# Turning the expert blocks' tokens with a DMA transpose instead of TensorE

## The reference, cut to what matters

```python
logits = x @ router_w + router_b
probs = jax.nn.softmax(logits, axis=-1)
top_v, top_i = jax.lax.top_k(probs, TOP_K)
top_v = top_v / jnp.sum(top_v, axis=-1, keepdims=True)
...
gate = jnp.einsum('td,edi->eti', x, gate_w) + gate_b[:, None, :]
up = jnp.einsum('td,edi->eti', x, up_w) + up_b[:, None, :]
h = jax.nn.silu(gate) * up
expert_out = jnp.einsum('eti,eid->etd', h, down_w) + down_b[:, None, :]
y = jnp.einsum('te,etd->td', weights, expert_out)
```

## Time and profile before

| what | us |
|---|---|
| median of 3 executions | 355.83 |
| lowest, highest | 355.47, 358.65 |
| the profiled execution | 359.83 |
| its span, first to last instruction | 358.0 |
| block 4's first matmul to block 38's first matmul | 144.10 |

### The profile page before, as it was taken

How to read it: one execution, slowest core, us unless ns; L and a number is a source line. 1 busy time by engine, 2 the same in 40 slices (tenths; PEclk the granted TensorE clock), 3 DMA queues, 4 the chain that set the end, 5 groups by cost and what they waited for, 6 DMA issues and landing times.

```text
span 358.0 us, 11098 instructions
## 1 busy us (share of the span) xinstructions
PE 295.7 (83%) x3773; PEld 178.3 (50%) x3774; DVE 276.0 (77%) x569; ACT 209.9 (59%) x380; POOL 202.7 (57%) x176
## 2 busy tenths in 40 slices
PE   0596868878878755977989989999999999899970
PEld 0186435545545532322446556666666666566640
DVE  3998785989999996778658767888888878688750
ACT  0277688989999964277135435555555555455520
POOL 2833132786889889452233476575756575565451
PEclk9998975989999997885599999999999999999995
DMA  7450100355544457679126777977768687767942
GB/s 183 84 180 3 61 2 6 117 187 171 185 168 142 152 168 226 234 221 240 37 53 112 114 124 123 134 127 125 132 119 134 116 149 109 128 120 131 116 63 30
DMA packets 70656, 45.00 MB, mean 126 GB/s; under 512 B 47992, under 2 KB 63608, under 8 KB 70240
## 3 DMA queue, kind: packets, MB, share of 16 engines
q1 hardware_dynamic: 62368, 34.09, 37.4%
q0 software_dynamic: 7488, 10.39, 20.3%
q10 hardware_dynamic: 768, 0.14, 0.3%
HBM read 23.43 MB, written 9.63 MB: 92 GB/s over the span
## 4 chain that ended last, share of the span: by engine, by line
PE 41%; DVE 16%; DMA 13%; issue 11%; ACT 9%; POOL 4%; POOLq 2%; ACTq 0%; DVEq 0%
PE bank L862 15%; DMA out_dram<-w_stage,gate 8%; PE bank L885 7%; DMA w_stage<-token_rows,gate 4%; ACT kq L1040 3%; PE bank L679 3%; DVE maxes L1327 3%; PE bank L762 2%; PE bank L588 2%; PE bank L850 2%; PE bank L670 2%; DVE s_exp L1336 2%; POOLq L527 2%; PE bank L552 2%; DMA w_exp<-in_L_conv_pairs_dram 1%
## 5 line engine op out<-in xcount | busy, mean ns | idle before, releaser
L862 PE MATMUL bank<-w_exp,v_t 128*128 x468 | 113.6, 379 | 2.0 <-DVE v_t L1526 1.4
L534 POOL DMA_INDIRECT out_dram<-w_stage,gate x39 | 62.2, 1594 | 54.4 <-DMA out_dram<-w_stage,gate 32.5
L862 PEld LDWEIGHTS bank<-w_exp,v_t 128*128 128x128 f16 x468 | 45.9, 98 | 42.2 <-issue 4.2
L885 PE MATMUL bank<-w_exp,kq 128*128 x468 | 57.9, 273 | 1.0 <-DVE w_stage L1572 0.8
L520 POOL DMA_INDIRECT w_stage<-token_rows,gate x39 | 40.1, 1029 | 27.9 <-ACT gate L1131 11.2
L1152 ACT ACTIVATE kq<-w_stage 128x512 f16<-128x512 f32 x38 | 23.9, 630 | 53.8 <-DVE w_stage L1555 53.8
L885 PEld LDWEIGHTS bank<-w_exp,kq 128*128 128x128 f16 x468 | 45.6, 98 | 15.0 <-issue 1.1
L438 POOL TENSOR_TENSOR w_exp<-w_stage,w_exp 128x1024 f16<-128x1024 f32 x16 | 34.1, 2134 | 12.3 <-ACT w_exp L1051 12.3
L1562 DVE TENSOR_TENSOR kq<-w_stage,kq 128x512 f16<-128x512 f32 x38 | 26.3, 693 | 16.7 <-ACT kq L1152 16.7
L1547 DVE TENSOR_TENSOR kq<-bank,v_t 128x512 f32<-128x512 f32 x39 | 26.9, 691 | 11.4 <-PE bank L862 11.3
L1555 DVE TENSOR_TENSOR w_stage<-s_exp,kq 128x512 f32<-128x512 f32 x39 | 27.1, 694 | 3.9 <-DVE kq L1547 0.4
(11 more groups left out here) (255 smaller groups left out, 519.2 us busy)
## 6 DMA issues: line engine op xcount, KB each, us to landing
w_stage<-in_L_ffn_gate_w_dram SPq DMA_DIRECT2D x8, 512.0 KB, 3.6
w_stage<-in_L_ffn_up_w_dram SPq DMA_DIRECT2D x8, 512.0 KB, 3.4
w_stage<-in_L_ffn_down_w_dram SPq DMA_DIRECT2D x8, 512.0 KB, 3.6
x_rows<-in_x_dram SPq DMA_DIRECT2D x8, 256.0 KB, 5.9
out_dram<-x_rows SPq DMA_DIRECT2D x4, 512.0 KB, 6.1
v_t<-in_L_ffn_up_b_dram SPq DMA_DIRECT2D x2, 1024.0 KB, 10.6
token_rows<-z_stack SPq DMA_DIRECT2D x4, 512.0 KB, 6.4
z_two<-z_stack SPq DMA_DIRECT2D x6, 256.0 KB, 2.4
```

The lines of the kernel that those rows point to most:

```text
L534: pool.indirect_dma_start(out, bass.IndirectOffsetOnAxis(t_scatter[:, b:b + 1], 0), yw[b % 2], None, compute_op=ALU.add).then_inc(s[f"y_la ...
L862: mm = pe.matmul(GU[par][k][:], xs[par][:, c, :], w_exp[:, w * W_EXP + k * W_PIECE + c * FF:][:, bass.ds(e, FF)], start=(n == 0), stop=(n ...
L885: mm = pe.matmul(YB[:, 0:L_COL], hs[par][:, c, :], w_exp[:, w * W_EXP + 2 * W_PIECE + c * L_COL:][:, bass.ds(e, L_COL)], start=(n == 0), s ...
```

## The change

Tokens are no longer turned by TensorE, save those of blocks 0 and 1. ScalarE and VectorE split a block's tokens as they lie, by rows, into one tile of 128 x 512 fp16 (high half, low half), and SyncE turns that tile with a third DMA transpose per block, issued after the two of the hidden product. There are four token buffers in place of two, and 6 gathers ahead in place of 5. On ScalarE `weigh` of n-3 moves behind `silu` of n, and tokens and share are those of block n+2. `yw` moves to another place in memory. The zeros are written by GpSimd itself, on the scatters' semaphores, whose counts all rise by one DMA; a scatter before which no scatter must have landed now waits for none (before, scatter 1 waited for scatter 0, and scatter 2 and all later ones for one scatter of each buffer).

```diff
-            sp.wait_ge(s["zero_ready"], 1)
-            for i in range(2):
-                sp.dma_start(out[TOKENS + SLOT * i:TOKENS + SLOT * (i + 1), :], ws_flat[:, 0:L_COL])\
-                    .then_inc(s["pad_out"], 16)
...
+            def turn_tokens(b):
+
+                sp.wait_ge(s["xl_ready"], b + 1)
+                sp.wait_ge(s["gu_ps"], 2 * (b - 1))
+                sp.dma_start_transpose(x_turned[b % 2], x_rows_h[b % 2]).then_inc(s[f"xt_in{b % 2}"], 16)
+
+            turn_tokens(2)
             for b in range(BLOCKS - 1):
                 turn_hidden(b)
+                if b + 3 < BLOCKS:
+                    turn_tokens(b + 3)
...
             table(pool.memset(ws_flat[:, 0:L_COL], 0.0))
-            pool.sem_inc(s["zero_ready"], 1)
+            for i in range(2):
+                pool.dma_start(out[TOKENS + SLOT * i:TOKENS + SLOT * (i + 1), :], ws_flat[:, 0:L_COL])\
+                    .then_inc(s[f"y_landed{i}"], 16)
...
             def gather(b):
 
-                if b >= 2:
-                    pool.wait_ge(s["share_ready"], b - 1)
-                pool.indirect_dma_start(xg[b % 2], None, token_rows,
+                if b >= 4:
+                    pool.wait_ge(s["share_ready"], b - 3)
+                    pool.wait_ge(s["xl_ready"], b - 3)
+                pool.indirect_dma_start(xg[b % 4], None, token_rows,
...
-                landed = [pool.value_load(t_landed[i][0:1, b:b + 1], min_val=16, max_val=8 * BLOCKS + 8)
-                          for i in range(2)] if b >= 2 else []
+                landed = [pool.value_load(t_landed[i][0:1, b:b + 1], min_val=16, max_val=8 * BLOCKS + 24)
+                          for i in range(2)] if b >= 1 else []
                 pool.wait_ge(s["y_ready"], b + 1)
-                if b == 1:
-                    pool.wait_ge(s["y_landed0"], 16)
...
-            for b in range(5):
+            for b in range(6):
                 gather(b)
             for b in range(BLOCKS):
-                if b + 5 < BLOCKS:
-                    gather(b + 5)
+                if b + 6 < BLOCKS:
+                    gather(b + 6)
...
-                if k == 0:
+                if k == 0 and first:
                     pe.wait_ge(s["xl_ready"], b + 1)
+                elif k == 0:
+                    pe.wait_ge(s[f"xt_in{par}"], 16 * turn)
...
-                hidden(n, par, 0, e1)
+                hidden(n, par, 0, e1, turn=turn)
                 if more:
-                    tokens_in(turn + par, 1 - par)
                     load_expert(n + 1, (k + 1) % 4)
...
+            def tokens_high(b):
+
+                act.wait_ge(s[f"x_got{b % 4}"], 16 * (b // 4 + 1))
+                if b >= 4:
+                    act.wait_ge(s[f"xt_in{b % 2}"], 16 * (b // 2 - 1))
+                act.activation(x_rows_h[b % 2][:, 0:L_COL], xg[b % 4][:, 0:L_COL], ACT.Copy)\
+                    .then_inc(s["xh_ready"], 1)
...
             for n in range(1, BLOCKS):
                 hidden_high(n - 1)
+                if n + 2 < BLOCKS:
+                    tokens_high(n + 2)
+                    share_of(n + 2)
+                silu(n, n % 2, first=(n == 1))
                 if n >= 3:
                     weigh(n - 3)
-                if n + 1 < BLOCKS:
-                    tokens_high(n + 1, (n + 1) % 2)
-                    share_of(n + 1)
-                silu(n, n % 2, first=(n == 1))
...
-                dve.tensor_scalar(t_landed[i], halves[i], 16.0, 16.0, ALU.mult, ALU.max).then_inc(s["landed_ready"], 1)
+                dve.tensor_scalar(t_landed[i], halves[i], 16.0, 16.0, ALU.mult, ALU.add).then_inc(s["landed_ready"], 1)
...
+            def tokens_low(b, k):
+
+                dve.wait_ge(s["xh_ready"], b + 1)
+                dve.tensor_tensor(x_rows_h[k % 2][:, L_COL:], xg[k][:, 0:L_COL], x_rows_h[k % 2][:, 0:L_COL],
                                   ALU.subtract).then_inc(s["xl_ready"], 1)
...
-                if more:
-                    tokens_low(n + 1, 1 - par)
+                if tokens:
+                    tokens_low(n + 2, (k + 2) % 4)
...
-            tokens_low(0, 0)
-            tokens_low(1, 1)
+            first_low(0)
+            first_low(1)
+            tokens_low(2, 2)
```

More of the change, by code:

```diff
@@ L167, in build @@
         ws_flat = w_stage[:].rearrange("p k w -> p (k w)")
+        an_flat = att_n[:].rearrange("p u c v -> p (u c v)")
         def two(flat, at, size, dt=None, parts=None):
@@ L175, in two @@
             return out2
[L177 to L181, removed]
+        xg = [ws_flat[:, ROW * i:ROW * (i + 1)] for i in range(4)]
+        x_turned = two(ve_flat, 0, 2 * P, fp16, 4)
+        x_hi, x_lo = ([t[:, 2 * i:2 * i + 2, :] for t in x_turned] for i in range(2))
+        x_rows_h = [t.bitcast(fp16) for t in two(an_flat, 0, 2 * P)]
+        y_sum = two(ws_flat, 4 * ROW, L_COL)
+        yw = two(z_two[:, 0, :].bitcast(fp32), 0, L_COL)
         h_sb = two(ws_flat, 2048, FF)
@@ L207, in build @@
         pad_rows = att_t[:, 336:336 + BLOCKS]
-        an_flat = att_n[:].rearrange("p u c v -> p (u c v)")
         at_flat = att
@@ L842, in weights_of, with first_tokens, hidden @@
                 return pe.snap(expert_reg[at], min_val=0, max_val=EXPERTS - 1) * (2 * W_EXP)
[L844 to L848, removed]
+            def first_tokens(k):
+                pe.wait_ge(s[f"x_got{k}"], 16)
+                if k == 1:
+                    pe.wait_ge(s["xl_ready"], 1)
                 for c in range(2):
-                    mm = pe.transpose(XT[:, P * c:P * c + P], xg[par][:, P * c:P * c + P], ident[:])
+                    mm = pe.transpose(XT[:, P * c:P * c + P], xg[k][:, P * c:P * c + P], ident[:])
                 mm.then_inc(s["xt_ps"], 1)
-            def hidden(b, par, k, e, first=False):
-                if k == 0:
+            def hidden(b, par, k, e, first=False, turn=None):
+                if k == 0 and first:
                     pe.wait_ge(s["xl_ready"], b + 1)
+                elif k == 0:
+                    pe.wait_ge(s[f"xt_in{par}"], 16 * turn)
                 if not first:
@@ L904, in _ @@
                 load_expert(b, b)
-            tokens_in(0, 0, first=True)
+            first_tokens(0)
             keep_warm(4)
@@ L909, in _ @@
             hidden(0, 0, 0, e0, first=True)
-            tokens_in(0, 1)
+            first_tokens(1)
             hidden(0, 0, 1, e0, first=True)
@@ L913, in _ @@
             hidden(1, 1, 0, e0, first=True)
-            tokens_in(1, 0)
             hidden(1, 1, 1, e0, first=True)
@@ L1159, in weigh @@
                 if b >= 2:
-                    act.wait_ge(s[f"y_landed{par}"], 16 * (b // 2))
+                    act.wait_ge(s[f"y_landed{par}"], 16 + 16 * (b // 2))
                 act.activation(yw[par], y_sum[par], ACT.Copy, scale=t_weight[:, bass.ds(b, 1)])\
                     .then_inc(s["y_ready"], 1)
-            tokens_high(0, 0, first=True)
+            first_high(0)
             share_of(0)
-            tokens_high(1, 1, first=True)
+            first_high(1)
             share_of(1)
+            tokens_high(2)
+            share_of(2)
             silu(0, 0, first=True)
@@ L1520, in _, with first_low @@
                 step(dve.tensor_copy(halves[i], ints))
-                dve.tensor_scalar(t_landed[i], halves[i], 16.0, 16.0, ALU.mult, ALU.max).then_inc(s["landed_ready"], 1)
-            def tokens_low(b, par, first=False):
+                dve.tensor_scalar(t_landed[i], halves[i], 16.0, 16.0, ALU.mult, ALU.add).then_inc(s["landed_ready"], 1)
+            def first_low(b):
                 dve.wait_ge(s["xh_ready"], b + 1)
-                dve.tensor_tensor(x_lo[par], bank[4][:, 0:L_COL].rearrange("p (c t) -> p c t", c=2), x_hi[par],
+                dve.tensor_tensor(x_lo[b], bank[4][:, 0:L_COL].rearrange("p (c t) -> p c t", c=2), x_hi[b],
+                                  ALU.subtract).then_inc(s["xl_ready"], 1)
+            def tokens_low(b, k):
+                dve.wait_ge(s["xh_ready"], b + 1)
+                dve.tensor_tensor(x_rows_h[k % 2][:, L_COL:], xg[k][:, 0:L_COL], x_rows_h[k % 2][:, 0:L_COL],
                                   ALU.subtract).then_inc(s["xl_ready"], 1)
@@ L1573, in down_bias, with dve_block @@
                     .then_inc(s["yadd_ready"], 1)
-            def dve_block(turn, k, first=0, more=True):
+            def dve_block(turn, k, first=0, more=True, tokens=True):
                 n, par = 2 * turn + k % 2, k % 2
@@ L1608, in _ @@
             dve_block(2, 1)
-            with dve.Fori(0, BODY - 1) as i:
+            with dve.Fori(0, BODY - 2) as i:
                 dve_block(2 * i + 3, 2)
@@ L1613, in _ @@
                 dve_block(2 * i + 4, 1)
-            dve_block(BLOCKS // 2, 2, more=False)
+            dve_block(BLOCKS // 2 - 2, 2)
+            dve_block(BLOCKS // 2 - 2, 3)
+            dve_block(BLOCKS // 2 - 1, 0)
+            dve_block(BLOCKS // 2 - 1, 1, tokens=False)
+            dve_block(BLOCKS // 2, 2, more=False, tokens=False)
```

20 lines of the change are left out of this document (9 added, 11 removed).

## The result

The changed kernel takes 368.05 us (median of 5 executions, 363.93 to 370.27) beside 358.52 us for the kernel before in the same session (355.47 to 359.2): ratio 1.0234, 95% interval 1.0171 to 1.0298. It is 2.3% slower; forecast was 352.0, 1.1% faster than the median then shown. The ratio leaves out two of the five executions, 370.11 and 370.27 us, which lie over 1.5% above the fastest, and the profile after is of the first of these, so it overstates the loss: its span is 10.3 us longer than the one before, where the ratio makes 8.4.

What follows compares the result with a forecast made beforehand. It took the two-block ring through scatter and gather, pace 4.05 us, as the new bound: -6.5 + 2.0 + 0.3 + 0.3 = -3.9 us, from the median 355.83 to 351.9, written 352.0; its own range 349 to 355, over all 345.5 to 361.0.

Steps and rivals of the forecast that it cites:

- TensorE's 3.89: TensorE in the 39 blocks: without the two token transposes a block costs 1.29 + 1.29 + 1.31 = 3.89 us.
- The DMA engines, 3.89 a block and no room: Gathers, scatters and three transposes ask all 16 engines for 3.89 us a block, leaving no room for idle moments.
- The ring: Weigh, scatter, gather, tokens, share, silu, weigh: 8.1 us for two blocks, pace 4.05, 6.5 us gained over 34 blocks.
- the boundaries: At 7 expert changes a scatter waits for the one before to land: 2.0 us lost together, between 0 and 7.
- The first blocks, +0.3: Start of the blocks: earlier token splitting delays the first gate bias, block 2 gains; +0.3 us, between -1 and +1.
- The zero rows, +0.3: GpSimd issues two more DMAs ahead of its tables, which VectorE needs: +0.3 us, between 0 and +1.5.
- C: In the blocks the two DMA queues take turns, transposes against gathers and scatters: pace 4.36, 360.5 us, chance 0.22.
- B: In the blocks TensorE sets the pace, gathers landing in about 3.2 us: pace 3.92, 346.0 us, chance 0.20.
- D: Pace 4.05, but each of the 7 expert boundaries costs a full 1.0 us: 357.0 us, chance 0.18.
- The sign that the prediction named for its own theory: ScalarE's `tokens_high` ends idle time made by a gather in most blocks; block starts 4.05 apart on average.
- Its sign of being wrong: TensorE waits for SyncE's third issue rather than a gather, or the stage outside the blocks moves over 1.5 us.

Runs made afterwards that it cites:

- the kernel without the traffic and with the long ring: Changed kernel with gathers eight ahead and SyncE signalling in place of the third transpose, against the kernel before: 350.22 us, ratio 0.9781.

## Why the prediction was wrong

*TensorE's 3.89: right.* Of the kernel without the traffic and with the long ring most blocks are 3.90 apart.

*The DMA engines, 3.89 a block and no room: wrong as a limit.* With the third transpose and eight ahead most blocks ran at 3.90 too. The price of the transpose there is 3.9 us over 34 blocks, by late landings here and there.

*The ring and the boundaries: the right mechanism, two terms too small.* This is the step that failed: a pace of 4.05 and 2.0 us for the boundaries, 139.6 us in all, where the 34 blocks took 151.93. The timelines give each term in the 28 turns that begin with the scatters of blocks 3 to 30. Means in us, the forecast's 2.0 for the boundaries spread over its 17 turns:

| term of a turn (two blocks) | forecast | changed kernel | without the third transpose |
|---|---|---|---|
| weighing's end to scatter | 0.28 + 0.12 | 0.71 | 0.67 |
| scatter to gather | 1.89 | 2.06 | 2.03 |
| gather's issue to use | 3.74 + 0.15 | 4.16 | 3.99 |
| use to the next weighing's end | 2.05 | 2.00 | 2.01 |
| sum | 8.23 | 8.93 | 8.70 |

The first row is 0.43 over its 0.28: 17 x 0.43 = 7.3 us of the 34 blocks are boundaries, where 2.0 were forecast. All of it falls on ten scatters, the five at a boundary (1.3 to 2.0 us after their weighing) and the five right behind these, which wait until GpSimd has issued the boundary's gather, as the scatter at 280.54 does; that second half the prediction did not see. The gather is 0.27 longer than forecast, 4.6 us in all. The prediction kept 3.74, "near the earliest of the late ones", though the earlier trace rows had shown 4.49 and 4.96 beside it, and in a ring every late gather counts. The gap from scatter to gather is 0.17 longer, 2.9 us. The 0.15 for the third transpose was right: taking it away shortens the gather by 0.17. This is an account of one execution of each kernel, not an experiment; that the ring as a whole makes the loss is what eight gathers ahead shows. With the ring of four, boundary scatters still wait and TensorE is busy all but 0.9 us: a longer ring swallows them, as the prediction said of the old one.

*The first blocks, +0.3: +1.0, and 0.8 more by the clock of block 0.* From block 1 to block 4 the changed kernel took 13.55 us, before 12.57. Without the third transpose it is 11.96, 0.6 less than before, so the reordering gained, within the prediction's range. The cost is the transposes beside the first gathers, to which the prediction gave no price. Block 0's 0.8 was in no sum, and where the clock rises is not the same in every execution: without the third transpose block 0 took 2.81 us with the ring of two and 3.73 with the ring of four.

*The zero rows, +0.3: nothing that can be measured.* The kernel with the exact waits alone had block 0 at 177.80, earlier than before (179.37). Kernels that differ from the changed one, up to block 0, at most in the number of gathers ahead had it between 176.31 and 180.54, so the 1.2 us of the first comparison are within the spread of executions.

*The rivals.* C came nearest, 360.5, with a ring of 8.7 (8.6 by its own terms, 7.96 - 3.74 + 4.4); but its reason, transposes that push the gather aside, is the smaller cause, 0.17 of a turn. B's engines were right, and without the third transpose and with a longer ring the time, 350.22, is nearer to B's. D had the boundaries at their size, 7.0 where the table makes 7.3. The sign that the prediction named for its own theory, `tokens_high` waiting for a gather in most blocks, came true; what was wrong was the forecast that the ring would still be shorter than 2 x 4.24. Its sign of being wrong, more than 1.5 us outside the 34 blocks, came true as well, with 10.3 - 7.8 = 2.5; the 0.8 of block 0 and the 1.2 ahead of it are spread between executions as far as the runs show.

The rule that the prediction quoted from the Trainium skill, DMA: Bandwidth & Descriptors, section on queues, rings and completion order (round-robin between queues, a whole packet at a time), led to C's time. The measurement gives it less: taking away all packets of the third transpose leaves the mean turn at 8.70 us, beside 8.93, and the gather at 3.99, beside 4.16.

## What to carry to other kernels

Before a consumer is moved earlier, count how many rounds the ring through the in-order queue then has (here GpSimd's scatter and the gather behind it), and size the ring by the late transfers of the profile, not by the earliest, and by what holds a transfer back in the queue, with the one behind it. A part that helps alone (exact waits, more buffers, 0.8% here) can be hidden in a change by another that costs four times as much (3.1% between that version and the changed kernel), so run the parts one by one. An experiment that adds the suspected load to the old kernel can point to the wrong cause; the four corners of two causes need only four kernels.

## What was not expected of the hardware

- The share of the DMA engines is no measure of room: 0.99 at 4.47 us a block and 1.00 at 4.06, with the same transfers, so that the same packets add up to 150 us of the 16 engines in one kernel and 138 in the other. In the kernel before with the extra transpose the share was 1.03, more than there is.
- Gathers of the same size land after 3.9 us in the median in the changed kernel, 3.9 without the third transpose, and 3.1 with four buffers and TensorE turning; by the page, which counts 8 of 32, 23 of 31 and 14 of 29. Over every gather whose landing the trace records the medians are 3.9, 3.7 and 3.3. Why was not found: in all three kernels a gather is issued 1.9 to 2.0 us (median) after a scatter on the same queue. The Trainium skill, DMA: Bandwidth & Descriptors, section on queues, rings and completion order, says that a completion signal lands only after every earlier write of its DMA engine, across queues: a gather behind a scatter would then wait for the scatter's writes. The traces agree in so far as every recorded gather between 200 and 340 us lands later than the scatter before it, by 0.26 us at the least. The difference between the kernels does not follow from it, as the scatter stands as near in each; no run here moves the gather away from its scatter.
- After TensorE had waited 2.48 us for a transpose, its granted clock was 0.61 in the next 4.4 us, between its levels of 1.2 and 2.4 GHz, and 12 matmuls took 4.45 us in place of 2.75. The length of the wait alone does not decide it: in the middle of the stage a wait of 1.64 us was followed by the same 4.45 (seven ahead, above), one of 1.83 us by 2.76 (blocks 2 and 3 turned by TensorE).
